# Third layer's attention: scores of batches 2 to 7 as three f32r products of upper and lower parts

## The chip, the cores and the metric

One core of a Trainium2 chip runs the whole program. The metric is device time in microseconds (us) for one execution, taken as the median of several. PE is TensorE (matmuls and transposes), DVE is VectorE, ACT is ScalarE, POOL is GpSimd, SP issues the transfers.

## The reference, cut to what matters

Four cross-attention layers run one after the other over x (8 batches x 256 rows x 256) and a context of 8 x 64 rows. The change lies in the last layer, which calls the function below twice, with its own weights each time, and then runs an MLP:

```python
def _cross_attention(q_in, kv_in, wq, bq, wk, bk, wv, bv, wo, bo, bias_k, bias_v):
    qh = (q_in @ wq + bq).reshape(b, q_len, H, K)        # 16 heads of 128
    kh = (kv_in @ wk + bk).reshape(b, t, H, K)           # 64 keys
    vh = (kv_in @ wv + bv).reshape(b, t, H, K)
    kh, vh = (each with one more row: bias_k, bias_v)
    logits = jnp.einsum('bqhk,bthk->bhqt', qh, kh) / sqrt(K)
    weights = jax.nn.softmax(logits, axis=-1)
    ctx = jnp.einsum('bhqt,bthk->bqhk', weights, vh).reshape(b, q_len, H * K)
    return ctx @ wo + bo

h = _layer_norm(x, ln1_scale, ln1_offset)
x = x + _cross_attention(h, xf_1, ...)                   # then the same with ln2 and the second weights
h = gelu(_layer_norm(x) @ w_fc1 + b_fc1) @ w_fc2 + b_fc2
return x + h
```

## The kernel before, in words

For each of the two attentions (a = 0, 1) the kernel first folds each head's weights into the context. `g3` (128 partitions x 2 halves of the 256 columns x 8 batches x 1024) is what a normalised row is multiplied with to give all 16 heads' scores against the 64 keys; `v3` is the same for the output. Only two large products are then left for each tile of 128 rows: scores, 128 x 256 by 256 x 1024, and output, 128 x 1024 by 1024 x 256. There are 16 tiles, two to a batch.

The function `attend` of each engine's program runs over these tiles in turns. Call turn n the body of `batch(i, ...)` for n = 2i + k. The engines do in turn n, in the order of the code:

- PE (L1184 on): `scores` of tile n+2 (L1159, four fp32 products of 512 columns, two instructions each, into four banks of PSUM that alternate by tile), `turn` of tile n (eight transposes of the weights, L1171), `turn_normed` of tile n+3 (transposes of the normalised rows, L1150), `rows_out` of tile n (L1180, 8 products of 256 columns).
- DVE: `stats` of tile n+4, `shifted` of tile n+2 (maximum L2002, the floor at zero L2004, subtraction L2005), `normed` of n+4 (L1994), `inverse` of n+2 (sum L2012, reciprocal L2013), `residual` of n (L2018).
- ACT: `copied` of tile n (transposed weights out of PSUM), `normed` of tile n+3 (transposed rows into `hT`), `weights` of n+2 (the exponential, L1226).
- POOL: `bias` of tile n (row plus output bias into `xb3`, L2313), `root3` of tile n+4 (L2089), `weights` of tile n+2 (times the reciprocal sum, L2307, 128 x 1024).

Each engine takes its instructions strictly in this order; semaphores tie the engines, with `wait(t, i, k)` for "step t of that tile is done". During the last eight turns of the second attention `feed` mixes in the first steps of the MLP: letters N (POOL: a root), A (ACT: upper parts of MLP weights), T (DVE, PE, ACT: one tile normalised, turned, copied), a (POOL: lower parts of MLP weights), X, x, C, c. In the turns with T, ACT's copies of the MLP's columns stand ahead of the exponential, and PE's transposes for them stand at the end of the turn.

A product "in parts" exists elsewhere in the kernel already: an fp32 matrix is held as an f32r upper part and an f32r remainder, and `PARTS = ((0, 0), (0, 1), (1, 0))` names the three products that are summed.

## Time and profile before

| | us |
|---|---|
| median of 3 runs | 1121.95 |
| lowest, highest | 1119.29, 1122.03 |
| span of the profiled execution | 1117.8 |
| median less that span | 4.15 |
| PE busy | 1043.6 (93%) |
| DVE busy | 725.0 (65%) |
| ACT busy | 601.4 (54%) |
| POOL busy | 451.9 (40%) |
| mean granted TensorE clock | 0.985 |

The span runs from the first to the last instruction of one profiled execution. An engine's busy time is the time in which at least one of its instructions ran; matmuls overlap, so the duration of one is longer than the distance to the next. The granted clock is 1 at 2.4 GHz and 0.5 at 1.2 GHz.

### The profile page before, as it was taken

To read this page: it belongs to the slowest core of one execution; us is meant where nothing else is said; L and a number is where in the kernel's file an instruction comes from. 1 tells how busy PE (TensorE), PEld (TensorE's weight loads), DVE (VectorE), ACT (ScalarE), POOL (GpSimd) and SP (SyncE) were. 2 spreads that over 40 slices of the span, in tenths; PEclk is the share of its full clock that TensorE was granted. 3 is DMA by queue.
4 is the path that set the end of the run, shared out by engine and by line. 5 is a ranking of instruction groups with operands and counts; after the bars stand their busy time and mean duration, and the time that the engine had idled before them with its cause. 6 is when DMAs were issued, how large, how long until landed. Compare 5 with 4: busy or idle time off the path is not lost.

```text
span 1117.8 us, 18511 instructions
## 1 busy us (share of the span) xinstructions
PE 1043.6 (93%) x6532; PEld 763.4 (68%) x6532; DVE 725.0 (65%) x1494; ACT 601.4 (54%) x1110; POOL 451.9 (40%) x436
## 2 busy tenths in 40 slices
PE   6889886799999989999999999999999999999998
PEld 4767764456665546777778866666788666667887
DVE  5868863567777734256478967666688776674553
ACT  3667765166665565455368742323587532346543
POOL 3768776434431123113034424334344243356241
PEclk9989999799999999999999999999999999999999
DMA  8010006777776021100023210000222200000000
GB/s 301 8 29 2 2 3 96 128 111 105 104 104 99 2 77 38 66 2 19 1 76 94 89 37 1 1 0 1 75 90 83 76 1 1 1 1 1 20 29 29
DMA packets 37152, 55.95 MB, mean 50 GB/s; under 512 B 12550, under 2 KB 29510, under 8 KB 34758
## 3 DMA queue, kind: packets, MB, share of 16 engines
q1 hardware_dynamic: 34998, 54.25, 21.8%
q8 instruction: 53, 0.87, 0.3%
q10 hardware_dynamic: 2064, 0.52, 0.2%
q14 instruction: 37, 0.30, 0.1%
HBM read 45.34 MB, written 9.18 MB: 49 GB/s over the span
## 4 chain that ended last, share of the span: by engine, by line
PE 69%; DVE 5%; ACT 3%; issue 2%; POOL 2%; DMA 1%; SPq 1%; ACTq 0%; DVEq 0%; POOLq 0%
PE ps L1180 9%; PE ps L900 8%; PE ps L1066 8%; PE ps L1159 7%; PE ps L970 5%; PE ps L851 4%; PE ps L1077 4%; PE ps L1087 4%; PE ps L818 4%; PE ps L752 3%; PE ps L971 3%; PE ps L832 2%; DVE nm L1748 2%; ACT pT L1223 1%; PE ps L870 1%
## 5 line engine op out<-in xcount | busy, mean ns | idle before, releaser
L1223 ACT ACTIVATE pT<-ps 128x512 f32<-128x512 f32 (+1 forms) x144 | 74.0, 558 | 150.9 <-PE ps L1171 119.1
L1748 DVE TENSOR_REDUCE nm<-ps 128x1 f32<-128x320 f32 x256 | 114.4, 486 | 54.1 <-PE ps L818 51.5
L1180 PE MATMUL ps<-v,pT 128*128 128x256 f32 x512 | 118.7, 385 | 7.0 <-DVE xr L2018 3.8
L2307 POOL TENSOR_TENSOR pn<-p,sm 128x1024 f32<-128x1024 f32 x32 | 60.9, 1904 | 151.5 <-DVE sm L2013 151.5
L2249 POOL TENSOR_TENSOR wl<-bun_m,wh 128x512 fp32r<-128x512 f32 x64 | 80.6, 1263 | 100.4 <-ACT wh L1223 100.4
L1159 PE MATMUL ps<-g,cT 128*128 128x512 f32 x256 | 114.8, 592 | 0.0
L1180 PEld LDWEIGHTS ps<-v,pT 128*128 128x128 f32 x512 | 94.6, 190 | 25.6 <-ACT pT L1223 11.9
L970 PE MATMUL ps<-wb,hid_high 128*128 128x512 f32 x256 | 97.0, 416 | 0.0
L1226 ACT ACTIVATE pT<-ps 128x512 f32<-128x512 f32 x160 | 85.3, 606 | 15.5 <-PE ps L832 15.3
L1226 ACT ACTIVATE p<-p 128x1024 f32<-128x1024 f32 (+1 forms) x64 | 68.5, 1070 | 41.5 <-DVE p L2005 40.0
L818 PE MATMUL ps<-ks,qs 97*128 97x320 bf16 x256 | 71.4, 311 | 15.1 <-DVE nm L1748 7.8
L1159 PEld LDWEIGHTS ps<-g,cT 128*128 128x128 f32 x256 | 48.2, 190 | 48.1 <-issue 46.9
L1833 DVE TENSOR_TENSOR hid_low<-hidf,hid_high 128x512 fp32r<-128x512 f32 x64 | 47.0, 735 | 42.9 <-ACT hid_high L1223 42.8
L971 PE MATMUL ps<-wb,hid_low 128*128 128x256 f32 x256 | 71.7, 280 | 0.0
L1425 ACT ACTIVATE hidf<-ps,vec 128x512 f32<-128x512 f32 x64 | 44.1, 689 | 43.5 <-PE ps L900 43.3
L2123 POOL TENSOR_TENSOR p<-p,mx 128x1024 f32<-128x1024 f32 x32 | 60.9, 1904 | 13.8 <-DVE mx L1691 13.8
L2265 POOL TENSOR_TENSOR xbm<-xr,row 128x256 f32<-128x256 f32 x32 | 23.5, 736 | 97.1 <-DVE xr L1860 92.2
L2012 DVE TENSOR_REDUCE sm<-p 128x16 f32<-128x1040 f32 x32 | 39.6, 1236 | 35.3 <-ACT p L1226 35.3
L2002 DVE TENSOR_REDUCE mx<-ps 128x16 f32<-128x1024 f32 x32 | 39.1, 1221 | 31.9 <-PE ps L1159 31.9
L970 PEld LDWEIGHTS ps<-wb,hid_high 128*128 128x128 f32 x256 | 48.1, 188 | 14.4 <-issue 4.8
L818 PEld LDWEIGHTS ps<-ks,qs 97*128 97x128 bf16 x256 | 23.2, 97 | 48.7 <-DVE nm L1748 25.2
L851 PE MATMUL ps<-pT,vt 128*32 128x256 f32 x768 | 48.1, 383 | 2.2 <-ACT oT L1223 2.2
(229 smaller groups left out, 2610.7 us busy)
## 6 DMA issues: line engine op xcount, KB each, us to landing
bun_m<-in_heads SPq DMA_DIRECT2D x32, 515.0 KB, 3.5
ks<-k_parts SPq DMA_DIRECT2D x48, 160.0 KB
qs<-q_parts SPq DMA_DIRECT2D x48, 128.0 KB
q_parts<-qp SPq DMA_DIRECT2D x8, 384.0 KB, 9.6
k_parts<-kp SPq DMA_DIRECT2D x8, 384.0 KB, 7.8
w<-in_w SPq DMA_DIRECT2D x2, 1024.0 KB, 4.8
xr<-in_x SPq DMA_DIRECT2D x1, 2048.0 KB, 15.9
out<-xr SPq DMA_DIRECT2D x16, 128.0 KB, 1.7
```

What stands on the lines that cost most here:

```text
L818: mm(ps[:, u % 2, 0:KEYS1], qs1[i % 3][0:MASK_ROW + 1, h, t * P:(t + 1) * P], ks1[i % 3][0:MASK_ROW + 1, h, :], start=True, stop=True).the ...
L851: last = mm(ps[32 * j:32 * j + 32, 5, 0:S], vt1[i % 2][:, c, h, :], p, start=c == 0, stop=c == 2)
L900: last = mm(ps[:, f % 2, :], w["wa"][a][:, kt, f * P:(f + 1) * P], w["x"][i % 2][b][:, kt, :], start=n == 0 and kt == 0, stop=n == len(PAR ...
L970: mm(ps[:, 2 + t, :], high, w["wb"][:, f, :, :].rearrange("p c d -> p (c d)"), start=f == 0, stop=False)
L971: last = mm(ps[:, 2 + t, 0:D], low, w["wb"][:, f, 0, :], start=False, stop=f == FT - 1)
L1066: last = mm(ps[:, bank, :], head_weights(m, a)["w" + name[0]][:, kt, :], cp3[b][:, kt, :], start=n == 0 and kt == 0, stop=n == len(PARTS) ...
L1159: last = mm(ps[:, 2 * t + c, :], hT[t][:, kt, :], g3[:, kt, bass.ds(b, 1), c * 512:(c + 1) * 512], start=kt == 0, stop=kt == KT - 1)
L1180: last = mm(o, pT3[half][:, n, :], v3[:, bass.ds(i, 1), 4 * half + n, :], start=half == 0 and n == 0, stop=half == 1 and n == 3)
L1223: return nc.scalar.activation(o, x, ACT.Identity, bias=bias, scale=scale)
L1226: return nc.scalar.activation(o, x, ACT.Exp, bias=bias, scale=scale)
L1748: v.tensor_reduce(nm1[i % 2][:, t, h:h + 1], ps[:, u % 2, 0:KEYS1], X, ALU.max, negate=True).then_inc(D1t["maxima"].sem, 1)
L2249: g.tensor_tensor(wl3[m % 2][:, cols], bun[m % BUNS][:, cols], wh3[m % 2][:, cols].bitcast(F32), ALU.subtract).then_inc(GH["low"].sem, 1)
```

## The change

The rows' transposes of batches 2 to 7 are kept as two f32r parts in `hs3`, laid over the memory of `cT`: ACT writes the upper part straight from PSUM, DVE subtracts it from PSUM for the lower (`normed_low`). `g3` of batch b is split as well: ACT copies its upper part into the place of batch b-2 (`g_high`, one half of the columns per turn, 128 x 1024), and POOL subtracts it from `g3` in place (`g_low`, also 128 x 1024). In POOL's turn n, `g_low` stands behind `weights`; PE's scores of batch b wait for the last `g_low` of that batch. With that, scores of batches 2 to 7 are 12 f32r products of 512 columns. Batches 0 and 1 stay fp32. The tile `xb3` goes: POOL adds the bias to the rows in place, as soon as the rows have been normalised.

```diff
--- before.py
+++ after.py
@@ -70,6 +70,7 @@
 BUNS = 3
 
 KEYS3 = H3 * SC
+PARTS3 = 2
 
 
 CONST = dict(ident=(0, P), quarter=(128, 4), parity=(132, 2), half=(134, 2), minus_half=(136, 1))
@@ -158,6 +159,9 @@
 
 
         xr = sb("xr", [P, NQ, D])
+        over_c = ExitStack()
+        hs3 = sb("hs3", [P, 2, 2, KT, P], F32R, where=over_c)
+        over_c.close()
         cT = sb("cT", [P, KT, C])
         cst = sb("cst", [P, NCONST])
         vec = sb("vec", [P, NVEC])
@@ -281,7 +285,10 @@
 
 
         late = ExitStack()
-        g3 = sb("g3", [P, KT, B, KEYS3], where=late)
+        over_g = ExitStack()
+        g3 = sb("g3", [P, KT, B, KEYS3], where=over_g)
+        over_g.close()
+        gs3 = sb("gs3", [P, KT, B, KEYS3], F32R, where=late)
         v3 = sb("v3", [P, B, HP, D], where=late)
         hn = [sb(f"hn{t}", [P, D], where=late) for t in range(2)]
         st3 = sb("st3", [P, 6], where=late)
@@ -289,7 +296,6 @@
         mx3 = [sb(f"mx3_{t}", [P, H3], where=late) for t in range(2)]
         sm3 = [sb(f"sm3_{t}", [P, H3], where=late) for t in range(2)]
         hT = [cT[:, t, 0:KT * P].rearrange("p (k n) -> p k n", k=KT) for t in range(2)]
-        xb3 = [cT[:, t, KT * P:KT * P + D] for t in range(2)]
         pT3 = [sb("pT3_0", [P, 4, P], where=late)]
         sb("beside_l2", [P, 72], where=late)
         bun_m3 = sb("bun_m3", [P, KT * F + FT * D], where=late)
@@ -401,9 +407,13 @@
 
 
         E3 = tallies("attn_pe", own_pe, normed=2, scores=2, turned_a=2, turned_b=2, out=2)
-        D3t = tallies("attn_dve", own_dve, stats=2, mean=2, eps=2, normed=2, max=2, floor=2, shifted=2, sum=2, inverse=2, rows=2)
-        A3 = tallies("attn_act", own_act, normed=2, weights=2, copied_a=2, copied_b=2)
-        G3 = tallies("attn_pool", own_pool, root=2, bias=2, weights=2)
+        D3t = tallies("attn_dve", own_dve, normed_low=2, stats=2, mean=2, eps=2, normed=2, max=2, floor=2, shifted=2, sum=2, inverse=2, rows=2)
+        A3 = tallies("attn_act", own_act, g_high=KT, normed=2, weights=2, copied_a=2, copied_b=2)
+        G3 = tallies("attn_pool", own_pool, g_low=KT, root=2, bias=2, weights=2)
+
+        def in_parts(t, a, b, k):
+
+            return t.at(a * (B - PARTS3) + b - PARTS3, k)
 
         def attn_end(t, a):
             return t.end((a + 1) * B)
@@ -1139,6 +1149,8 @@
                 def turn_normed(i, k, first=False):
                     wait(D3t["normed"], i, k)
                     wait(A3["normed"], i, k - 1)
+                    if i + (k - 1) // 2 >= PARTS3:
+                        pe.wait_ge(D3t["normed_low"].sem, in_parts(D3t["normed_low"], a, i + (k - 1) // 2, (k - 1) % 2))
                     if first:
                         for t in (DH["out"], AH["out"]):
                             pe.wait_ge(t.sem, t.end((a + 1) * H3))
@@ -1154,9 +1166,17 @@
                     t, b = k % 2, i + k // 2
                     wait(A3["normed"], i, k)
                     wait(D3t["shifted"], i, k - 2)
-                    for c in range(2):
+                    if b >= PARTS3:
+                        pe.wait_ge(D3t["normed_low"].sem, in_parts(D3t["normed_low"], a, b, t))
+                        pe.wait_ge(G3["g_low"].sem, in_parts(G3["g_low"], a, b, KT - 1))
+                        for c in range(2):
+                            for n, (p, q) in enumerate(PARTS):
+                                for kt in range(KT):
+                                    last = mm(ps[:, 2 * t + c, :], hs3[:, t, p, kt, :], gs3[:, kt, b if q else b - PARTS3, c * 512:(c + 1) * 512],
+                                              start=n == 0 and kt == 0, stop=n == len(PARTS) - 1 and kt == KT - 1)
+                    for c in range(0 if b >= PARTS3 else 2):
                         for kt in range(KT):
-                            last = mm(ps[:, 2 * t + c, :], hT[t][:, kt, :], g3[:, kt, bass.ds(b, 1), c * 512:(c + 1) * 512],
+                            last = mm(ps[:, 2 * t + c, :], hT[t][:, kt, :], g3[:, kt, b, c * 512:(c + 1) * 512],
                                       start=kt == 0, stop=kt == KT - 1)
                     last.then_inc(E3["scores"].sem, 1)
 
@@ -1195,6 +1215,7 @@
                             if move == "T":
                                 if k + 3 < left:
                                     wait(A3["normed"], i, k + 3)
+                                    pe.wait_ge(D3t["normed_low"].sem, in_parts(D3t["normed_low"], a, i + (k + 3) // 2, (k + 3) % 2))
                                 mlp_turn(0, tile, bank=6)
 
                 pe.wait_ge(D2["rows"].sem, D2["rows"].end(NQ))
@@ -1550,11 +1571,16 @@
                 def normed(i, k):
                     wait(E3["normed"], i, k)
                     wait(E3["scores"], i, k - 2)
-                    copy(hT[k % 2][:, :, :], ps[:, 6, 0:D].rearrange("p (k n) -> p k n", k=KT)).then_inc(A3["normed"].sem, 1)
+                    o = hs3[:, k % 2, 0, :, :] if i + k // 2 >= PARTS3 else hT[k % 2][:, :, :]
+                    copy(o, ps[:, 6, 0:D].rearrange("p (k n) -> p k n", k=KT)).then_inc(A3["normed"].sem, 1)
 
                 def weights(i, k):
                     wait(D3t["shifted"], i, k)
                     exp(p3[k % 2][:, :, :], p3[k % 2][:, :, :], scale=SCALE3).then_inc(A3["weights"].sem, 1)
+
+                def g_high(b, kt):
+                    wait(E3["scores"], b - PARTS3, 1)
+                    copy(gs3[:, kt, b - PARTS3, :], g3[:, kt, b, :]).then_inc(A3["g_high"].sem, 1)
 
                 def copied(i, k):
                     wait(E3["out"], i, k - 1)
@@ -1575,6 +1601,8 @@
                                 mlp_columns(0, t, bank=6)
                         if k + 2 < left:
                             weights(i, k + 2)
+                        if i + PARTS3 < B:
+                            g_high(i + PARTS3, k)
                         if a == 0 and i == B - 2:
                             rounded(H3, k)
                         for move, n in feed(a, i, k):
@@ -2012,10 +2040,16 @@
                     own3("sum", i, k, v.tensor_reduce(sm3[t][:, :], p3[t][:, :, :], X, ALU.add))
                     v.reciprocal(sm3[t][:, :], sm3[t][:, :]).then_inc(D3t["inverse"].sem, 1)
 
+                def normed_low(i, k):
+                    t = k % 2
+                    wait(A3["normed"], i, k)
+                    v.tensor_tensor(hs3[:, t, 1, :, :], ps[:, 6, 0:D].rearrange("p (k n) -> p k n", k=KT),
+                                    hs3[:, t, 0, :, :].bitcast(F32), ALU.subtract).then_inc(D3t["normed_low"].sem, 1)
+
                 def residual(i, k):
                     wait(E3["out"], i, k)
                     wait(G3["bias"], i, k)
-                    v.tensor_tensor(rows(i, k), ps[:, 7, 0:D], xb3[k % 2], ALU.add).then_inc(D3t["rows"].sem, 1)
+                    v.tensor_tensor(rows(i, k), ps[:, 7, 0:D], rows(i, k), ALU.add).then_inc(D3t["rows"].sem, 1)
 
                 def batch(i, left=NQ):
                     for k in range(2):
@@ -2028,6 +2062,8 @@
                                 mlp_normed(0, t)
                         if k + 4 < left:
                             normed(i, k + 4)
+                        if k + 3 < left and i + (k + 3) // 2 >= PARTS3:
+                            normed_low(i, k + 3)
                         if k + 2 < left:
                             inverse(i, k + 2)
                         residual(i, k)
@@ -2308,9 +2344,14 @@
                                     ).then_inc(G3["weights"].sem, 1)
 
                 def bias(i, k):
-                    wait(D3t["rows"], i, k - 2)
+                    wait(D3t["normed"], i, k)
                     settle(pool)
-                    g.tensor_tensor(xb3[k % 2], xq(i, k), vs3[:, :], ALU.add).then_inc(G3["bias"].sem, 1)
+                    g.tensor_tensor(xq(i, k), xq(i, k), vs3[:, :], ALU.add).then_inc(G3["bias"].sem, 1)
+
+                def g_low(b, kt):
+                    pool.wait_ge(A3["g_high"].sem, in_parts(A3["g_high"], a, b, kt))
+                    g.tensor_tensor(gs3[:, kt, b, :], g3[:, kt, b, :], gs3[:, kt, b - PARTS3, :].bitcast(F32), ALU.subtract
+                                    ).then_inc(G3["g_low"].sem, 1)
 
                 def batch(i, left=NQ):
                     for k in range(2):
@@ -2319,6 +2360,8 @@
                             root3(i, k + 4)
                         if k + 2 < left:
                             weights(i, k + 2)
+                        if i + PARTS3 < B:
+                            g_low(i + PARTS3, k)
                         if a == 0 and (i, k) in ((B - 2, 1), (B - 1, 0)):
                             low(H3, 1 - k)
                         for move, t in feed(a, i, k):
```

## Rows read from the trace of the kernel before

**Rows 1.** Page, part 4: the chain that ended last, shares by engine.
```profile
PE 69%; DVE 5%; ACT 3%; issue 2%; POOL 2%; DMA 1%; SPq 1%; ACTq 0%; DVEq 0%; POOLq 0%
```

**Rows 2.** Timeline of PE, first attention, turn 4: start, us, engine, line, out<-in, count.
```profile
694.99 3.60 PE L1159 MATMUL ps<-g,cT 128*128 128x512 f32 x8
...
699.77 3.72 PE L1180 MATMUL ps<-v,pT 128*128 128x256 f32 x16
```

**Rows 3.** Timeline of DVE in the same turn; in brackets idle time before, and releaser.
```profile
698.62 1.23 DVE L2002 TENSOR_REDUCE mx<-ps 128x16 f32<-128x1024 f32 x1 [1.89 <-PE ps L1159]
...
700.10 1.23 DVE L2005 TENSOR_TENSOR p<-ps,p 128x1024 f32<-128x1024 f32 x1
...
702.46 1.24 DVE L2012 TENSOR_REDUCE sm<-p 128x16 f32<-128x1040 f32 x1 [0.82 <-ACT p L1226]
```

**Rows 4.** Timeline of POOL in the same turn.
```profile
704.06 1.90 POOL L2307 TENSOR_TENSOR pn<-p,sm 128x1024 f32<-128x1024 f32 x1 [5.24 <-DVE sm L2013]
705.92 0.72 POOL L2313 TENSOR_TENSOR cT<-xr,vs 128x256 f32<-128x256 f32 x1
```

**Rows 5.** The chain that ended last in order of time: start, us, engine, line, count.
```profile
463.05 10.90 PE ps L900 x48
...
695.15 3.43 PE ps L1159 x8
```

**Rows 6.** Groups by line and form: busy us in total, mean ns, idle before.
```profile
L2232 POOL TENSOR_TENSOR xp_low<-xc,xp_high 128x1024 fp32r<-128x1024 f32 x4 | 9.5, 2386 | 25.9 <-DVE xp_high L1802 25.9
...
L1223 ACT ACTIVATE cp_high<-cT 128x1024 fp32r<-128x1024 f32 x1 | 1.1, 1059 | 0.0
...
L2018 DVE TENSOR_TENSOR xr<-ps,cT 128x256 f32<-128x256 f32 x32 | 11.8, 369 | 18.6 <-PE ps L1180 12.5 <-POOL cT L2313 6.0
```

**Rows 7.** Timelines of DVE, PE and POOL, first attention, turns 1 and 2.
```profile
676.61 0.46 DVE L2004 TENSOR_SCALAR p<-mx 128x16 f32<-128x16 f32 x1
...
678.31 3.60 PE L1159 MATMUL ps<-g,cT 128*128 128x512 f32 x8
...
674.44 1.90 POOL L2307 TENSOR_TENSOR pn<-p,sm 128x1024 f32<-128x1024 f32 x1 [2.91 <-DVE sm L2013]
676.30 0.73 POOL L2313 TENSOR_TENSOR cT<-xr,vs 128x256 f32<-128x256 f32 x1
...
681.06 1.91 POOL L2307 TENSOR_TENSOR pn<-p,sm 128x1024 f32<-128x1024 f32 x1 [3.53 <-DVE sm L2013]
```

**Rows 8.** Timelines of PE and ACT, second attention, turns 8 to 12.
```profile
958.17 3.60 PE L1159 MATMUL ps<-g,cT 128*128 128x512 f32 x8
...
975.06 3.60 PE L1159 MATMUL ps<-g,cT 128*128 128x512 f32 x8
...
993.49 3.60 PE L1159 MATMUL ps<-g,cT 128*128 128x512 f32 x8
...
975.96 1.07 ACT L1226 ACTIVATE p<-p 128x1040 f32<-128x1040 f32 x1
```

**Rows 9.** PE's longest idle time in the middle of the kernel, in PE's timeline.
```profile
196.59 0.71 PE L818 MATMUL ps<-ks,qs 97*128 97x320 bf16 x2 [5.92 <-DMA ks<-k_parts]
```

**Rows 10.** Stretches: from:to, length, busy PE PEld DVE ACT POOL, granted clock, DMA.
```profile
32.00:34.00 2.00, 1.97 (x34) 1.64 (x36) 0.94 (x1) 0.36 (x2) 2.00 (x2) 0.93 0.03 8
34.00:37.00 3.00, 3.00 (x20) 2.77 (x19) 2.40 (x6) 0.99 (x3) 1.59 (x2) 0.50 0.00 0
37.00:40.00 3.00, 2.85 (x40) 2.28 (x39) 2.97 (x3) 2.56 (x5) 1.11 (x2) 0.98 0.01 3
...
76.00:84.00 8.00, 7.91 (x48) 6.48 (x49) 4.03 (x5) 4.99 (x11) 2.67 (x3) 0.50 0.00 0
...
192.00:194.00 2.00, 0.00 (x0) 0.00 (x0) 0.57 (x1) 0.00 (x0) 1.84 (x3) 1.00 1.22 139
194.00:196.00 2.00, 0.00 (x0) 0.00 (x0) 0.00 (x0) 0.00 (x0) 1.71 (x3) 0.54 0.71 100
...
204.00:206.00 2.00, 1.34 (x6) 0.35 (x4) 1.57 (x4) 1.47 (x3) 0.00 (x0) 0.90 0.81 98
```

## Prediction

> **What bounds the kernel now.** I read the chain that ended last first: PE carries 69% of it [rows 1], and in both attentions it consists of L1159 and L1180 by turns. Then I laid the timelines of four engines over one turn. PE goes without a gap through 3.43 us of scores [rows 5] and 1.35 us of transposes up to 699.77, then 3.56 us of output [rows 2]; from turn 2 to turn 4 pass 694.99 - 678.31 = 16.68 us [rows 2, 7], 8.34 a turn. The other engines wait for PE.
>
> What the totals hide is the length of the softmax chain behind one tile's scores. With T for the start of the scores in a turn: maximum at T+3.63, subtraction at T+5.11, sum at T+7.47 [rows 3], POOL's product with the reciprocals at T+9.07, and the next POOL instruction can start at T+10.93 [rows 4]. So each tile's chain ends in the following turn. It costs nothing before, since PE transposes these weights only two turns after it computed the scores. POOL idles 5.24 us of a turn [rows 4], but it does so in front of this product.
>
> **Scores in parts.** Fp32 scores take 3.43 us a tile (x8 in the chain) [rows 5]. The MLP's f32r products of the same shape, 512 columns with new weights each, take 10.90/48 = 0.227 us [rows 5]. Twelve are 2.73 us: 0.70 us less a tile, and a turn of PE falls from 8.34 to 7.64. Batches 2 to 7 are 12 tiles, 24 in both attentions: 16.8 us, if PE goes on without gaps. The last product's tail of 0.17 us behind its distance stays.
>
> **The split of the rows.** ACT's copy only changes its target's type. DVE's subtraction is 128 x 256 from PSUM, 0.37 us as L2018 [rows 6], between `normed` and the sum. DVE waits there for the exponential, 0.82 us [rows 3], and that hides it; uncovered it would be 0.37 on the chain below. The bounds for the whole item are 0 and 12 x 0.37 = 4.4 us.
>
> **The split of g3.** Each of turns 0 to 11 of an attention gets one ACT copy of 128 x 1024, 1.06 us, and one POOL subtraction of 128 x 1024 into f32r, 2.39 us [rows 6]. The ACT copy stands behind the exponential, which ends at T+7.4, and has nothing behind it before the next turn's transposes. POOL's load is no trouble either: of 5.24 us idle [rows 4] the shorter turn leaves 4.5. The place in the order is the trouble. PE's scores in turn n+1 (n odd) are the first of a new batch and wait for the `g_low` of turn n. This stands in POOL's queue behind the product with the reciprocals, which ends the chain of the tile whose scores PE computed in the same turn n. So PE can't begin turn n+1 before that whole chain has run, and one `g_low` on top of it.
>
> **The price of one such wait.** With the shorter scores everything moves up by 0.70: the product on POOL would start at T+8.37. One thing pushes it back. The even turn's `g_low` begins some 10.2 us after the start of that turn and ends 12.65 us after it, at T+5.0 of the odd turn, and DVE's floor (L2004, a tensor_scalar, due at T+4.2) falls into it. Such a collision shows in [rows 7]: the floor was issued at 676.61 while POOL's bias ran from 676.30 to 677.03, and took 0.46; in turn 4 all that lies between maximum and subtraction is 0.25 [rows 3]. So subtraction starts at about T+5.10, like before, and POOL's product at T+9.06. Plus 1.86, plus 2.39, plus some 0.04: PE starts the next turn at T+13.35 in place of T+8.34. That leaves PE idle for 13.35 - 7.64 = 5.7 us.
>
> The Trainium skill, SBUF — State Buffer, section "Who interferes with whom", has the rule for the collision: DVE in a two-port mode and GpSimd exclude each other for a whole instruction, and tensor_scalar can be such a DVE instruction. The trace agrees (0.46 us there). By that rule an added GpSimd instruction of 2.39 us can block DVE for as long.
>
> **The sum without the clock.** Attention 1: two turns take 7.64 + 13.35 = 20.99 in place of 16.68, +4.3, for turns 2 to 11, five pairs: +21.6. The first wait is longer. In turn 1 DVE is still behind: POOL's product of turn 0 starts at 674.44 and that of turn 1 at 681.06 [rows 7]. `g_low` fills 676.30 to 678.69 and holds the floor from 676.61 until then; subtraction 678.75, exponential 680.0, sum 681.1, product 682.7, `g_low` 684.6 to 686.95. Turn 2 starts at 687.0 instead of 678.31 [rows 7]: +8.7. Turns 12 and 13 have fast scores and no wait: -1.4. Sum +28.9.
>
> Attention 2: +8.7 and three pairs of 4.3 (12.9) alike. In turn 9 `feed` puts ACT's columns ahead of the exponential, and these wait for PE's transposes at the end of the turn: the exponential comes at 975.96, 0.90 us behind the start of PE's turn 10 at 975.06 [rows 8]. That was harmless; now it is in the chain. With PE's work of turn 9 ending at T+7.87 the exponential starts at T+8.77, sum T+9.87, product T+11.5, `g_low` ends at T+15.7: the pair takes 7.64 + 15.75 = 23.4 for 975.06 - 958.17 = 16.89 [rows 8], +6.5. In turn 11 the root for the MLP stands behind turn 10's `g_low` too, which pushes the transposes to about T+10 and the end to T+17.9: 8.0 + 17.9 = 25.9 for 993.49 - 975.06 = 18.43, +7.5. With -1.4 for turns 12 and 13: +34.2.
>
> Both: +63. Bounds: without collisions of the floor and with everything else hidden, 12 waits less 0.7 each, +55; with 0.7 more each, +71.
>
> **The clock.** Before, PE is never idle in the attentions for more than 2 us, and the clock stays at 1. A wait of 5.7 us and more, twelve times, is new. The nearest row is PE's idle time of 5.92 us up to 196.59 [rows 9]: the clock is 1 until 194, 0.54 over 194 to 196, so it fell some 3.5 us into the idle time, and it came back only after 204 [rows 10]. Ours would be at 1.2 GHz (0.5) when PE resumes. How long it stays there: around 34 it fell after a poor stretch and was back at 37, five us after PE had resumed at 32; the one at 76 to 84 stayed at half for over 8 us of nearly full work [rows 10]. I take 5 us at half, since our work is dense from the resumption on, as after 32: 2.5 us lost a wait, 12 x 2.5 = 30. The lost time lies on the path, since PE's even turn is paced by PE. Bounds: 0 if the clock doesn't fall, 12 x 4.9 = 59 by the long row.
>
> The Trainium skill, TensorE: Matmul & The Clock Gate, section "HAM oscillation — how this bites in real kernels", describes a kernel that waits in every tile and starts each cold again; that rule speaks against this change, and the rows above agree with it for one wait (0.54 and then 0.50).
>
> **In place of `xb3`** POOL adds the bias to the rows in place behind the wait for `normed`, four turns old in its start: no instruction more or less, 0. SP issues nothing new. PE's added waits for the rows' lower parts are met: that subtraction ends some 1 us before the scores that use it.
>
> **Forecast.** The profiled execution: 1117.8 + 63 + 30 = 1210.8; the median stood 4.15 above the span: 1215 us, with 1200 to 1232 as its own range. Chance 0.75.
>
> **Rivals.**
> - The clock holds. The waits are as priced, but PE stays at 2.4 GHz: 1121.95 + 63 = 1185, between 1177 and 1193. For it: the idle times of up to 2 us in the attentions leave the clock at 1. Against: the row of 5.92 us. Chance 0.12.
> - The clock is worse, each resumption like that at 76: 1121.95 + 63 + 59 = 1244, 1232 to 1250. Chance 0.06.
> - The other side: PE stays the bound. The lower parts would have to be ready when PE gets to the new batch, that is `g_low` would have to end before T+7.64 of the odd turn. It decides at that point; I find T+13.3. POOL's 5.24 us of idle time would hold 2.39 us, if it ran there. Only if POOL's order or the semaphore's count were not what I read does the price turn to a gain: 1121.95 - 16.8 = 1105 (1101 to 1112). Chance 0.04.
> - It doesn't do what it says: twelve f32r products take as long as eight fp32 instructions, and low parts come in time: 1122. With the waits it would be some 1121.95 + 63 + 30 + 10 x 2 x 0.7 = 1229, inside the forecast's range. For the first, 0.03.
>
> **How the numbers follow.** The likeliest case gives 1215. The range takes in the first rival and the second up to 1244: 1176 to 1244, with 0.93 of the chances laid out, less some room for my sizes. A change of 0.3%, 3.4 us, is about what a measurement of this kernel can tell from none. Faster 0.04, same 0.03, slower 0.93.
>
> **What would show it.** In the changed trace: twelve f32r matmuls of L1159's successor in 2.7 us in a turn at full clock; PE idle for 5 to 6 us ahead of the scores of turns 4, 6, ... 12, 8.7 ahead of those of turn 2, released by POOL's subtraction into `g`; 20 to 23 us a pair of turns; POOL's subtraction starting right behind its product; the granted clock at 0.5 for some us after each wait, and nowhere else new. If PE shows no idle time there, the order was misread and the time is 1105. If the pairs take 21.0 us with a clock of 1, the first rival holds.

## The result, and the profile after

The changed kernel takes 1214.12 us (median of 4 runs, 1211.31 to 1220.13); the kernel before, run beside it, 1121.57 (1119.29 to 1122.03). The ratio is 1.082, 95% interval 1.078 to 1.086. The forecast was 1215 us, slower. The profiled execution is the longest of the four, 1220.13 us, with a span of 1218.2.

In the page of the changed kernel the chain that ended last (shares of the span by engine) has 57% of PE for 69% in [rows 1], 10% of POOL for 2%, and 10% of "issue", time in which the engine waited for nothing that the profile shows, for 2%. Below are two groups of the page (busy us, mean ns, idle time before and its releaser) and the longest entry of the view of waits (us in total, times, longest):

```profile
PE 57%; issue 10%; POOL 10%; DVE 4%; ACT 2%; DMA 1%; SPq 1%; POOLq 0%; ACTq 0%; DVEq 0%
...
L1175 PE MATMUL ps<-gs,hs 128*128 128x512 f32 x288 | 99.4, 510 | 75.8 <-POOL gs L2353 75.8
...
L2353 POOL TENSOR_TENSOR gs<-g,gs 128x1024 fp32r<-128x1024 f32 x24 | 56.7, 2361 | 0.0
```
```profile
PE ps L1175 <- POOL gs L2353: 75.8, 12, 8.6
```

L1175 is the f32r scores, L2353 is `g_low`. PE waits for it twelve times, 75.8 us in all: six batches in each attention, as the order of the queues has it.

The timeline of PE in the first attention, turns 2 to 5 (start, us, engine, line; L1200 is the output):

```profile
693.00 5.46 PE L1175 MATMUL ps<-gs,hs 128*128 128x512 f32 x12 [8.55 <-POOL gs L2353]
...
699.79 3.72 PE L1200 MATMUL ps<-v,pT 128*128 128x256 f32 x16
703.16 3.11 PE L1175 MATMUL ps<-gs,hs 128*128 128x512 f32 x12
...
707.45 3.72 PE L1200 MATMUL ps<-v,pT 128*128 128x256 f32 x16
716.55 5.46 PE L1175 MATMUL ps<-gs,hs 128*128 128x512 f32 x12 [5.38 <-POOL gs L2353]
...
723.50 3.72 PE L1200 MATMUL ps<-v,pT 128*128 128x256 f32 x16
726.87 3.12 PE L1175 MATMUL ps<-gs,hs 128*128 128x512 f32 x12
```

To be seen: the odd turn's scores (703.16) go on without a gap, and the next even turn starts 13.39 us after them. The same twelve products take 3.11 us without a wait ahead of them and 5.46 behind this one (4.34 to 5.46 behind the twelve waits). The windows of the same stretch tell why (us; busy us and count of PE, PEld, DVE, ACT, POOL; granted clock; DMA share; GB/s):

```profile
692.00:698.00 6.00, 5.00 (x12) 3.96 (x13) 0.00 (x0) 0.00 (x0) 2.05 (x3) 0.50 0.00 0
698.00:704.00 6.00, 5.91 (x31) 4.97 (x30) 4.91 (x8) 3.38 (x5) 0.06 (x1) 0.95 0.00 0
704.00:716.00 12.00, 7.07 (x36) 5.61 (x34) 7.01 (x15) 3.38 (x5) 9.16 (x6) 0.99 0.01 2
716.00:722.00 6.00, 5.45 (x13) 4.21 (x14) 0.00 (x0) 0.00 (x0) 1.59 (x3) 0.50 0.00 0
```

When PE resumes, the granted clock is 0.50, that is 1.2 GHz of 2.4, and it stays there for some three to five and a half us, behind each of the twelve waits.

POOL in turn 3 shows the queue order at work. The first `g_low` is that of the even turn 2, the second the one that PE waits for; it starts right behind the product (L2343), and PE resumes 0.14 us after it (716.41 to 716.55):

```profile
703.94 1.91 POOL L2343 TENSOR_TENSOR pn<-p,sm 128x1024 f32<-128x1024 f32 x1 [9.89 <-DVE sm L2041]
705.81 2.36 POOL L2353 TENSOR_TENSOR gs<-g,gs 128x1024 fp32r<-128x1024 f32 x1
...
712.21 1.90 POOL L2343 TENSOR_TENSOR pn<-p,sm 128x1024 f32<-128x1024 f32 x1 [2.84 <-DVE sm L2041]
714.07 2.34 POOL L2353 TENSOR_TENSOR gs<-g,gs 128x1024 fp32r<-128x1024 f32 x1
```

DVE's floor (L2032) under such a `g_low`, in turn 1 and in turn 3:

```profile
682.59 2.07 DVE L2032 TENSOR_SCALAR p<-mx 128x16 f32<-128x16 f32 x1
...
706.30 1.23 DVE L2030 TENSOR_REDUCE mx<-ps 128x16 f32<-128x1024 f32 x1 [1.36 <-PE ps L1175]
707.56 0.65 DVE L2032 TENSOR_SCALAR p<-mx 128x16 f32<-128x16 f32 x1
708.24 1.22 DVE L2033 TENSOR_TENSOR p<-ps,p 128x1024 f32<-128x1024 f32 x1
```

Its 16 elements a partition take 2.07 us in turn 1, since it ends with POOL's subtraction (682.28 to 684.62), and 0.65 in turn 3, to 708.21, with the one that began at 705.81. The subtraction behind it, from PSUM, keeps its 1.22 us beside POOL's next instruction, the bias; e9 below has it beside `g_low` itself (705.37, 1.23 us).

Where the 100.4 us between the spans of 1218.2 and 1117.8 went: the last output of attention 1 on PE, in the kernel before and then in the changed one:

```profile
784.61 3.72 PE L1180 MATMUL ps<-v,pT 128*128 128x256 f32 x16 [0.31 <-ACT pT L1223]
```
```profile
833.45 3.72 PE L1200 MATMUL ps<-v,pT 128*128 128x256 f32 x16 [0.31 <-ACT pT L1244]
```

These are 48.8 us. Of them 6.0 were there before the attention began (its first scores start at 658.9 for 652.94): this one execution had a lower clock in stages where nothing was changed (0.86 for 1.00 from 100 to 150 us, 0.74 for 0.83 from 190 to 230). So attention 1 costs 42.9 and all behind it 51.5.

### The profile page after: what moved, and what is told of

Same layout as the page of the kernel before. It is cut to its first block, busy times and chain, and to the rows that moved or that the text cites. A ratio compares the mean times of both kernels' runs of the same rounds, so it can differ in the third digit from the quotient of the medians.

```text
span 1218.2 us, 18809 instructions
## 1 busy us (share of the span) xinstructions
PE 1066.4 (88%) x6628; PEld 805.4 (66%) x6628; DVE 742.8 (61%) x1518; ACT 624.1 (51%) x1134; POOL 508.1 (42%) x460
## 4 chain that ended last, share of the span: by engine, by line
PE 57%; issue 10%; POOL 10%; DVE 4%; ACT 2%; DMA 1%; SPq 1%; POOLq 0%; ACTq 0%; DVEq 0%
PE ps L910 7%; PE ps L1076 7%; PE ps L1175 6%; PE ps L980 5%; POOL gs L2353 4%; PE ps L861 4%; PE ps L1087 4%; PE ps L1097 4%; POOL pn L2343 4%; PE ps L828 3%; PE ps L762 3%; PE ps L1200 2%; PE ps L981 2%; PE ps L842 2%; DVE nm L1776 2%
## 5 line engine op out<-in xcount | busy, mean ns | idle before, releaser
L1175 PE MATMUL ps<-gs,hs 128*128 128x512 f32 x288 | 99.4, 510 | 75.8 <-POOL gs L2353 75.8
L2343 POOL TENSOR_TENSOR pn<-p,sm 128x1024 f32<-128x1024 f32 x32 | 60.9, 1904 | 190.3 <-DVE sm L2041 190.3
L1175 PEld LDWEIGHTS ps<-gs,hs 128*128 128x128 f32 x288 | 71.1, 253 | 96.6 <-issue 79.9
L1200 PE MATMUL ps<-v,pT 128*128 128x256 f32 x512 | 118.7, 385 | 8.0 <-DVE xr L2052 4.4
L1200 PEld LDWEIGHTS ps<-v,pT 128*128 128x128 f32 x512 | 94.6, 190 | 26.6 <-ACT pT L1244 12.9
L1247 ACT ACTIVATE pT<-ps 128x512 f32<-128x512 f32 x160 | 85.3, 606 | 15.5 <-PE ps L842 15.2
L1247 ACT ACTIVATE p<-p 128x1024 f32<-128x1024 f32 (+1 forms) x64 | 68.2, 1068 | 45.6 <-DVE p L2033 44.7
L2301 POOL TENSOR_TENSOR xbm<-xr,row 128x256 f32<-128x256 f32 x32 | 23.5, 736 | 97.0 <-DVE xr L1888 92.1
L2040 DVE TENSOR_REDUCE sm<-p 128x16 f32<-128x1040 f32 x32 | 39.6, 1236 | 30.7 <-ACT p L1247 30.7
L2353 POOL TENSOR_TENSOR gs<-g,gs 128x1024 fp32r<-128x1024 f32 x24 | 56.7, 2361 | 0.0
```

The lines of the kernel that those rows point to most:

```text
L1175: last = mm(ps[:, 2 * t + c, :], hs3[:, t, p, kt, :], gs3[:, kt, b if q else b - PARTS3, c * 512:(c + 1) * 512], start=n == 0 and kt == 0, ...
L1200: last = mm(o, pT3[half][:, n, :], v3[:, bass.ds(i, 1), 4 * half + n, :], start=half == 0 and n == 0, stop=half == 1 and n == 3)
L1247: return nc.scalar.activation(o, x, ACT.Exp, bias=bias, scale=scale)
L2343: g.tensor_tensor(pn3[t][:, :, :], p3[t][:, :, 0:SC], sm3[t][:, :].unsqueeze(2).broadcast_to([P, H3, SC]), ALU.mult).then_inc(G3["weights" ...
L2353: g.tensor_tensor(gs3[:, kt, b, :], g3[:, kt, b, :], gs3[:, kt, b - PARTS3, :].bitcast(F32), ALU.subtract).then_inc(G3["g_low"].sem, 1)
```

## The experiments

In each diff `-` is the changed kernel unless another is named. Every run stands beside runs of the kernel before on the same chip.

**e1: both halves of the split ahead of the softmax chain.** If the place in the queues is the cause, this removes the waits.

```diff
@@ ACT, batch()
                     for k in range(2):
+                        if i + PARTS3 < B:
+                            g_high(i + PARTS3, k)
                         copied(i, k)
...
-                        if i + PARTS3 < B:
-                            g_high(i + PARTS3, k)
@@ POOL, batch()
                     for k in range(2):
+                        if i + PARTS3 < B:
+                            g_low(i + PARTS3, k)
...
-                        if i + PARTS3 < B:
-                            g_low(i + PARTS3, k)
```

> The changed kernel with ACT's upper copy and POOL's lower subtraction of g3 moved to the head of their turns; nothing else is touched. My theory (place in POOL's order): the subtraction of an odd turn then ends some 5 us into the turn, before PE's 7.64 us are over, PE has no gap, the clock stays at 1, and the 24 faster scores are left: 1121.6 - 16.8 = 1105 us (1101 to 1111). Rival A (the splitting costs by its load on ACT, DVE and POOL or by collisions, wherever it stands): above 1121. Rival B (f32r products gain nothing here): 1120 to 1123.

Measured: 1134.23 us (1132.96 to 1136.05), ratio 1.010 (1.008 to 1.012). 80 of the 93 us are back, so the place of the two halves of the split caused most of the loss. The 17 us of gain are not there: of the expectations the first rival came, costs of load or collisions wherever the split stands. PE, DVE and POOL in a turn:

```profile
703.09 3.00 PE L1175 MATMUL ps<-gs,hs 128*128 128x512 f32 x12 [0.34 <-DVE hs L2046]
...
711.35 2.98 PE L1175 MATMUL ps<-gs,hs 128*128 128x512 f32 x12 [0.35 <-DVE hs L2046]
```
```profile
703.29 1.24 DVE L2040 TENSOR_REDUCE sm<-p 128x16 f32<-128x1040 f32 x1 [0.46 <-ACT p L1247]
...
707.39 1.77 DVE L2032 TENSOR_SCALAR p<-mx 128x16 f32<-128x16 f32 x1
...
711.55 1.24 DVE L2040 TENSOR_REDUCE sm<-p 128x16 f32<-128x1040 f32 x1 [0.46 <-ACT p L1247]
```
```profile
704.90 1.91 POOL L2343 TENSOR_TENSOR pn<-p,sm 128x1024 f32<-128x1024 f32 x1 [2.85 <-DVE sm L2041]
706.76 2.36 POOL L2353 TENSOR_TENSOR gs<-g,gs 128x1024 fp32r<-128x1024 f32 x1
```

At the head of POOL's turn `g_low` is in effect right behind the product of the turn before. There it holds DVE's floor until 709.16, as the exclusion of DVE and POOL that the prediction priced would have it. That closes a loop of its own: sum 703.29, product 704.90, `g_low` 706.76, floor to 709.16, shifted scores 709.19, exponential, next sum 711.55. It is 8.26 us long with no step of PE in it, where PE's work is 7.64 and was 8.34 [rows 2, 7]: nearly all of the 0.70 us a tile goes into it. In attention 2 the turns with the MLP's rows take up to 11.96 us.

**e2: only POOL's order, `g_low` between the root and the product.**

```diff
@@ POOL, batch()
                             root3(i, k + 4)
+                        if i + PARTS3 < B:
+                            g_low(i + PARTS3, k)
                         if k + 2 < left:
                             weights(i, k + 2)
-                        if i + PARTS3 < B:
-                            g_low(i + PARTS3, k)
```

> The changed kernel with POOL's subtraction ahead of its product with the reciprocals, but ACT's copy still behind the exponential. Theory: PE now waits for subtraction, exponential, ACT's copy and POOL's subtraction: next turn at T+10.2 in place of T+13.2, so PE idles 2.5 us in place of 5.4. If the clock holds through 2.5 us: some 19 us above the kernel before, 1141 (1130 to 1150). If it falls there too, another 12 x 2.4: 1165 to 1170. Rival (POOL's order does not matter, its load does): 1214.

Measured: 1171.1 us (1169.73 to 1177.79), ratio 1.044 (1.041 to 1.047), just above the 1165 to 1170 that stood for waits that still cost clock. POOL's order alone gives 43 us back; the 37 us between this kernel and e1 are the price of ACT's place once POOL's is cured. ACT's copy remains behind the exponential, and `g_low` waits for it, so PE idles for 2.5 us. PE's scores behind three such waits:

```profile
706.84 4.48 PE L1175 MATMUL ps<-gs,hs 128*128 128x512 f32 x12 [2.48 <-POOL gs L2353]
...
726.43 3.00 PE L1175 MATMUL ps<-gs,hs 128*128 128x512 f32 x12 [2.46 <-POOL gs L2353]
...
744.49 4.57 PE L1175 MATMUL ps<-gs,hs 128*128 128x512 f32 x12 [2.50 <-POOL gs L2353]
```

With the same idle time the clock fell at two of these and held at one. Four of this kernel's twelve waits are longer (5.31 to 5.48 us), and all four are followed by slow scores (4.82 to 5.46 us). Of the eight of 2.45 to 2.87 us five are (4.47 to 4.59 us), and three are not (2.99 to 3.01 us).

**e3: only ACT's order, `g_high` at the head of its turn** (the ACT half of e1's diff).

> The changed kernel with ACT's upper copy at the head of its turn, POOL's order as in the change. Theory: the copy is not what PE waits for, since POOL is busy with the product until after it; so no change: 1214 (1208 to 1220), PE's idle time of about 5.3 us a pair of turns stays. Rival (ACT's copy is the late link): 1105 to 1145.

Measured: 1215.52 us (1214.05 to 1219.38), ratio 1.083 (1.080 to 1.085), no change. The waits stay at 75.9 us, twelve times. In the order of the change ACT's place costs nothing, since POOL's queue is the later of the two links; e2 against e1 shows that it is the next one.

**e4: the waits kept, PE kept busy in them** by six fp32 products of 512 columns into the bank that the scores overwrite.

```diff
@@ PE, scores()
+                        if t == 0:
+                            for n in range(FILL):
+                                mm(ps[:, 2 * t, :], ident, v3[:, 0, 0:2, :].rearrange("p h d -> p (h d)"), start=True, stop=True)
                         pe.wait_ge(G3["g_low"].sem, in_parts(G3["g_low"], a, b, KT - 1))
```

> The changed kernel with six added fp32 products of 512 columns (0.86 us each, 5.1 us together, results overwritten) in each of the twelve places in which PE waits. The chain on the other engines stays as long. If the clock's fall costs what I put down, 2.0 to 2.7 us a wait, it holds now and the time falls by 24 to 30 us: 1187 (1182 to 1194), granted clock at 1 in the attentions. If the slow scores after the wait are due to something else than idle time, 1214.

Measured: 1191.49 us (1189.69 to 1196.65), ratio 1.062 (1.059 to 1.064): 22.6 us less than the changed kernel, with 0.972 to 0.983 as mean clock for 0.942 to 0.951. Two even turns of it (L1179 is the scores there, and the rest of the wait stands in brackets):

```profile
709.83 3.06 PE L1179 MATMUL ps<-gs,hs 128*128 128x512 f32 x12 [0.30 <-POOL gs L2357]
...
730.89 3.06 PE L1179 MATMUL ps<-gs,hs 128*128 128x512 f32 x12 [0.30 <-POOL gs L2357]
```

The pair takes 21.06 us at full clock, where 23.55 pass in the changed kernel (693.00 to 716.55). This splits the loss. By the medians, each with some 3 or 4 us either way, 22.6 of 92.6 us are clock and 70 waiting, less what the shorter scores give. The traces are sharper, since the stages before the attentions can be left out: from the first scores of attention 1 to the end the kernel before takes 464.9 us, e4 533.0 and the changed kernel 559.3. One wait of e4 was not covered (2.54 us idle, scores of 4.62 us, about 1.6 lost). That makes some 66.5 us of waiting and 27.9 of clock.

**e5: the scores of batches 2 to 7 as fp32 products of the upper parts.** All splits and waits stay; the lower parts are left out of the scores, so that they are coarser.

```diff
@@ PE, scores()
-                            for n, (p, q) in enumerate(PARTS):
-                                for kt in range(KT):
-                                    last = mm(ps[:, 2 * t + c, :], hs3[:, t, p, kt, :], gs3[:, kt, b if q else b - PARTS3, c * 512:(c + 1) * 512],
-                                              start=n == 0 and kt == 0, stop=n == len(PARTS) - 1 and kt == KT - 1)
+                            for kt in range(KT):
+                                last = mm(ps[:, 2 * t + c, :], hs3[:, t, 0, kt, :].bitcast(F32), gs3[:, kt, b - PARTS3, c * 512:(c + 1) * 512].bitcast(F32),
+                                          start=kt == 0, stop=kt == KT - 1)
```

> The changed kernel with all its waits and splits, but the scores of batches 2 to 7 as four fp32 products of the upper parts (the lower parts' products are left out, so what is computed is less exact). Theory: fp32 scores are 0.70 us longer in each of 24 turns, and all of it lies on the path: 1214 + 17 = 1231 us (1225 to 1236). Rival (f32r products gain nothing, or the gain is swallowed by the wait): 1214.

Measured: 1228.4 us (1223.86 to 1231.16), ratio 1.097 (1.095 to 1.100): 14.3 us above the changed kernel. So the f32r products do save time on the path, and the rival in which they save nothing falls. The expectation had all of the 16.8 us on the path, 0.70 in each of 24 turns; the trace has less, 10.3 us from the first scores to the end (569.6 for 559.3). DVE, POOL and PE in turn 3 (L2031 is the floor there, L2352 `g_low`, L1174 the scores):

```profile
702.39 0.18 DVE L2031 TENSOR_SCALAR p<-mx 128x16 f32<-128x16 f32 x1
...
700.09 2.35 POOL L2352 TENSOR_TENSOR gs<-g,gs 128x1024 fp32r<-128x1024 f32 x1
...
697.49 3.60 PE L1174 MATMUL ps<-gs,hs 128*128 128x512 f32 x8
```

With the longer scores the floor is due at 702.39, when `g_low` is all but over (702.44), and takes 0.18 us; it ends 5.08 us after the start of the scores. With the shorter ones it is due earlier and is held, to 5.05 us after that start (708.21 - 703.16). In attention 1 such a turn takes 13.41 to 13.68 us to the next scores in e5 and 13.24 to 13.80 in the changed kernel. So in the odd turns that a wait follows the faster product saves next to nothing (in attention 2 the five of them are 1.4 us longer in e5, all together). The other 14 turns give 9.8 us at full clock.

**e6: on the kernel before, only the bias added in place.**

```diff
@@ DVE, residual()
-                    v.tensor_tensor(rows(i, k), ps[:, 7, 0:D], xb3[k % 2], ALU.add)
+                    v.tensor_tensor(rows(i, k), ps[:, 7, 0:D], rows(i, k), ALU.add)
@@ POOL, bias()
-                    wait(D3t["rows"], i, k - 2)
+                    wait(D3t["normed"], i, k)
-                    g.tensor_tensor(xb3[k % 2], xq(i, k), vs3[:, :], ALU.add)
+                    g.tensor_tensor(xq(i, k), xq(i, k), vs3[:, :], ALU.add)
```

> The kernel before with only one part of the change: POOL adds the bias to the rows in place behind the wait for the normalised rows, and the tile for the sum goes. Theory: no time, 1121.3 (1118 to 1125). Rival (the freed wait lets POOL run ahead and collide with DVE, or shortens the end): more than 3 us either way.

Measured: 1121.83 us for 1123.02, ratio 0.999 (0.997 to 1.001). This part costs nothing that can be measured.

**e8: ACT's columns for the MLP behind the exponential**, in attention 2.

```diff
@@ ACT, batch()
                             normed(i, k + 3)
+                        if k + 2 < left:
+                            weights(i, k + 2)
                         for move, t in feed(a, i, k):
...
-                        if k + 2 < left:
-                            weights(i, k + 2)
```

> The changed kernel with ACT's columns of the MLP behind the exponential in the four turns that have them. Theory: turn 9 of the second attention loses the 2.9 us by which the exponential waited for PE's transposes; turn 11 little, since DVE's sum stands there behind the MLP's row, which waits for POOL. 1211 (1206 to 1214). Rival (the exponential sets both): 6 us less, 1208 or below.

Measured: 1208.47 us (1204.25 to 1213.74), ratio 1.079 (1.076 to 1.082), 5.7 us less than the changed kernel, between the two expectations, and by its interval of about 3 us either way the median doesn't tell them apart. The trace does (scores of turns 10 and 12):

```profile
1053.05 5.46 PE L1175 MATMUL ps<-gs,hs 128*128 128x512 f32 x12 [5.28 <-POOL gs L2353]
...
1077.84 5.18 PE L1175 MATMUL ps<-gs,hs 128*128 128x512 f32 x12 [5.34 <-POOL gs L2353]
```

Turns 8 and 9 take 23.5 us (from 1029.57) for 25.6 in the changed kernel, turns 10 and 11 24.8 for 30.7, together 8.0 us less. So the rival holds: ACT's order sets both pairs, and the second more than the first.

**e9: `g_high` at the head of ACT's turn, `g_low` behind bias and root, and there only after DVE's floor.**

```diff
@@ POOL, batch() (ACT as in e3)
                             root3(i, k + 4)
+                        if i + PARTS3 < B:
+                            wait(D3t["floor"], i, k + 2)
+                            g_low(i + PARTS3, k)
                         if k + 2 < left:
                             weights(i, k + 2)
-                        if i + PARTS3 < B:
-                            g_low(i + PARTS3, k)
```

> Of the kernel with both steps ahead (1134 us) the trace shows turns of 8.25 us in a closed loop: DVE's floor waits 1.6 us for POOL's subtraction to end, and PE waits 0.35 us for the rows' lower part. Here POOL's subtraction stands behind bias and root and waits for the floor. Theory (the collision makes the loop): the floor takes 0.2 us again, turns come down to 7.9 to 8.1, the time to 1120 (1113 to 1128). Rival (the loop is POOL's load, whatever collides): 8.25 or longer, 1134 or above.

Measured: 1123.46 us (1119.84 to 1131.83), ratio 1.002 (0.999 to 1.004). DVE's floor and PE's turn:

```profile
705.15 0.18 DVE L2032 TENSOR_SCALAR p<-mx 128x16 f32<-128x16 f32 x1
```
```profile
700.83 3.02 PE L1175 MATMUL ps<-gs,hs 128*128 128x512 f32 x12
...
708.50 3.02 PE L1175 MATMUL ps<-gs,hs 128*128 128x512 f32 x12
```

The floor takes 0.18 us instead of 1.77, and a turn of PE 7.67 without a gap, against 8.26 in e1. The rival in which POOL's load makes the loop is out, since POOL's work is the same; so it was the collision. The edit moves `g_low` behind bias and root and adds the wait; what each does alone was not tried. Two things keep the time at that of the kernel before: turn 1 of each attention takes 12.2 us for 8.9, since PE waits 2.11 us for `normed_low`, and turns 9 to 12 of attention 2 take 8.5, 11.7, 11.9 and 8.8 us.

**e10: e9, and on DVE `normed_low` right behind the shifted scores, `normed` behind the sum.**

```diff
@@ DVE, against e9
-                        if k + 4 < left:
-                            normed(i, k + 4)
                         if k + 3 < left and i + (k + 3) // 2 >= PARTS3:
                             normed_low(i, k + 3)
-                        if k + 2 < left:
-                            inverse(i, k + 2)
+                        inverse(i, k + 2, k + 2 < left, k + 4 < left)
@@ inverse(), between the sum and the reciprocal
+                    if more:
+                        normed(i, k + 2)
```

> The same, and DVE subtracts the rows' lower part right behind the scores' subtraction and normalises the next rows only behind the sum. Theory: PE no longer waits for the lower part, turns of 7.65 to 7.8 us, 1113 (1107 to 1120), faster than the kernel before. Rival (DVE and POOL together need more than 7.9 us a turn in any order): 1120 and above.

Measured: 1119.24 us (1115.39 to 1124.46), ratio 0.998 (0.996 to 1.000); 1113 (1107 to 1120) was expected. The turns of attention 1 are the 7.67 us that the theory had; turns 10 to 12 of attention 2 still take 12.0, 12.1 and 9.1 us. POOL, DVE, PE and ACT there (L1822 normalises the MLP's rows, L895 transposes them on PE, the ACT line adds their columns, L1247 is the exponential):

```profile
975.81 2.34 POOL L2354 TENSOR_TENSOR gs<-g,gs 128x1024 fp32r<-128x1024 f32 x1
...
975.87 2.43 DVE L1822 TENSOR_SCALAR hnm<-xr,mvm 128x256 f32<-128x256 f32 x1
978.22 0.41 DVE L2050 TENSOR_TENSOR hs<-ps,hs 128x256 fp32r<-128x256 f32 x1
...
978.73 0.66 PE L895 MATMUL ps<-cst,hnm 128*128 128x128 f32 x2 [3.69 <-DVE hs L2050]
979.04 5.30 PE L1175 MATMUL ps<-gs,hs 128*128 128x512 f32 x12
...
979.43 0.81 ACT L1244 ACTIVATE xc<-ps,vec 128x128 f32<-128x128 f32 x2 [7.52 <-PE ps L895]
980.13 1.06 ACT L1247 ACTIVATE p<-p 128x1040 f32<-128x1040 f32 x1
```

A second tensor_scalar of DVE, L1822, is held by `g_low` for 2.43 us; PE's transposes wait for the `normed_low` behind it, ACT's columns for these, the exponential for the columns, and POOL's next product for the exponential. The scores were complete long before. Behind PE's 3.69 us of idle time its clock is at half as well (5.30 us).

**e11: e10, and the columns behind the exponential** (e8's diff on top).

> The kernel with rows late (1119 us), and ACT's columns of the MLP behind the exponential. In its trace turns 10 to 12 of the second attention take 12.0, 12.1 and 9.1 us, since DVE's row for the MLP (tensor_scalar) waits up to 2.4 us for POOL's subtraction. Theory: the exponential is not what is late there, so only some 2 us: 1117 (1114 to 1120).

Measured: 1109.43 us (1107.8 to 1114.44) for 1123.02, ratio 0.987 (0.984 to 0.991). It is faster than both kernels. ACT and PE in the same turns:

```profile
974.06 1.07 ACT L1247 ACTIVATE p<-p 128x1040 f32<-128x1040 f32 x1 [1.57 <-DVE p L2033]
```
```profile
976.83 0.41 PE L895 MATMUL ps<-cst,hnm 128*128 128x128 f32 x2 [1.33 <-DVE hs L2050]
```

The exponential follows the shifted scores directly, PE idles 1.33 us instead of 3.69, and turns 10 to 12 take 9.5, 9.5 and 7.9 us where e10 has 12.0, 12.1 and 9.1. Those 6.4 us are most of the 9.8 between the two medians. Expected was 1117 (1114 to 1120), on the theory that the exponential is not what is late in these turns. That was wrong: it is, here as in e8.

**e12: e11, and the MLP's rows (L1822) ahead of the floor**, that is before `g_low` may start.

```diff
@@ DVE, against e11
-                            shifted(i, k + 2)
-                        for move, t in feed(a, i, k):
-                            if move == "T":
-                                mlp_normed(0, t)
+                            shifted(i, k + 2, lambda: [mlp_normed(0, t) for move, t in feed(a, i, k) if move == "T"])
```

> The same, and DVE's row for the MLP between maximum and floor, ahead of POOL's subtraction in place of behind its start. Theory: it no longer collides, turns 10 to 12 take 8 to 9 us, 7 to 8 us less: 1110 (1106 to 1115). Rival (POOL's added work in these turns sets them, whatever collides): 1116 to 1119 as without it.

Measured: 1110.51 us (1109.15 to 1113.47), ratio 0.988 (0.985 to 0.991), the same as e11. The time agrees with the expectation, its reason doesn't: against e11 the step gained nothing that the medians show. L1822 does fall from 2.45 to 0.8 us, and turn 10 from 9.5 to 7.9, but turns 11 and 12 stay at 9.5 and 7.9: `g_low` starts later for it, and PE waits 0.85 us for that in turn 11.

## Why the prediction was right

**The order on POOL.** The prediction rests on one reading: `g_low` of an odd turn stands behind the product that ends the chain of the tile scored in the same turn. The trace has twelve waits with that releaser, and of the moves ACT's alone gives nothing back (e3), POOL's alone 43 us (e2) and both 80 (e1): POOL's place is the link that decides, as predicted, and ACT's, which the prediction took for harmless, is the next behind it. The rival in which PE stays the bound needed lower parts in time; even when they are (e1), it comes to 1134 and not 1105, since the floor then sits behind `g_low`. Only with that cured too (e9 to e11) is part of the gain seen.

**The size of a wait.** From an odd turn's start to the next even one 13.35 us were predicted, 13.39 and 13.24 (726.87 to 740.11) came, and 13.53 to 13.80 in the later turns of attention 1. The pair without the clock was 20.99, and e4 shows 21.06. The first wait was put at 8.7 us later than before: PE was at 693.00 in this execution, which is 687.0 as predicted plus the 6.0 from earlier stages. The steps in between held as well: in turn 3 the subtraction starts at T+5.08 (708.24 - 703.16) where T+5.10 was taken, and POOL's product at T+9.05 (712.21 - 703.16) for T+9.06.

**Attention 2.** Turns 8 and 9 took 25.6 us (1035.52 to 1061.12) where 23.4 + 2.5 were predicted. Turns 10 and 11 took 30.7 for 25.9 + 2.5, so this term was 2.3 too small. The timeline of DVE, PE and ACT in turn 11:

```profile
1082.77 0.41 DVE L2022 TENSOR_SCALAR hn<-xr,mv 128x255 f32<-128x255 f32 x1 [1.12 <-POOL mv L2125]
1083.10 0.42 DVE L2046 TENSOR_TENSOR hs<-ps,hs 128x256 fp32r<-128x256 f32 x1
...
1083.61 0.41 PE L895 MATMUL ps<-cst,hnm 128*128 128x128 f32 x2 [3.88 <-DVE hs L2046]
1091.81 5.46 PE L1175 MATMUL ps<-gs,hs 128*128 128x512 f32 x12 [7.78 <-POOL gs L2353]
...
1084.76 1.06 ACT L1247 ACTIVATE p<-p 128x1040 f32<-128x1040 f32 x1
```

I had the MLP's transposes at T+10, held by the root behind `g_low`. They came at T+11.76 (1083.61 - 1071.85). The root of the rows themselves stands even further back in POOL's queue, DVE's `normed` waits 1.12 us for it, `normed_low` stands behind `normed`, and PE's transposes behind that. I had called PE's waits for the rows' lower parts met; in this turn one was not, and e10 shows the same path. What makes it dear is the place of ACT's columns ahead of the exponential: without it the two turns take 24.8 us (e8).

**The scores.** 2.73 us a tile was right for the timeline (3.0 to 3.1 with the tail). The 16.8 us of saving were counted for a PE without gaps. Behind waits less comes, and the sum had this right, with the subtraction at T+5.10 "like before" in an odd turn: the floor's collision takes the 0.70 us back, and e5's trace shows it. The rival with 1229 us counted both turns of each pair and so was some 7 us too high. Without the waits 13.6 of the 16.8 us came (e11).

**The clock.** The mechanism was right at every wait. Even turns of attention 1 took 10.16, 10.32, 8.89, 9.55, 9.94 and 10.01 us where they take 7.57 to 7.62 in e4, at full clock: 13.3 us lost, 2.2 a wait where 2.5 were taken, 15 in all. Attention 2 lost 14.5 by the same comparison, which makes 27.8 for the kernel, as the 27.9 from the stretches of e4; the 30 of the sum was some 2 us too high. The price of one wait lies between 1.3 and 2.8 us. The rival in which the clock holds is out: its time is nearly that of e4, 1191, and 1177 to 1193 was its range.

The Trainium skill, TensorE: Matmul & The Clock Gate, section "HAM oscillation — how this bites in real kernels", says that a kernel which waits in each of its tiles starts every tile cold. This trace agrees in all twelve cases (clock 0.50 when PE resumes).

**The sum.** Predicted +28.9 + 15 for attention 1 and +34.2 + 15 behind it, 93.1; the profiled execution shows 42.9 and 51.5, 94.4. By kind, 63 of waiting and 30 of clock were predicted, and some 66.5 and 27.9 came: the waits were priced too low, in turns 10 and 11 above all, and the clock too high. That the total came out within 1.3 us, and the median on the forecast's 1215, is in part luck. The median rose by 92.6. My way from span to median was wrong, though it did no harm: I added 4.15 us to the span of the kernel before, while the changed kernel's own time stands 1.93 above its span. The 4.15 was mostly scatter between executions of the kernel before (1119.29 to 1122.03), whose times stand 1.8 above their spans wherever both are on record (1120.08 for 1118.3).

## What to carry to other kernels

Before an operation is put into an in-order queue, ask what stands ahead of it there and whose consumer it feeds: 2.4 us of work on an engine with 5 us of slack in a turn cost 93 us in all, because it stood behind the end of a chain that its own consumer had started. When such work is moved, look a second time at what it now collides with, since e1 swapped one wait for a closed loop of 8.26 us; a place behind the floor and the release of two more orders (e10, e11) then brought 13.6 of the 16.8 us counted. A faster PE product is worth what the slowest loop beside it leaves: next to nothing in the odd turns of the changed kernel (e5) and in e1. So lay that loop out first.

## What was not expected of the hardware

- The clock fell at five of eight waits of only 2.45 to 2.87 us, and held at three (e2). In the attentions of the kernel before, idle times of up to 1.9 us had left it at 1. But in e9 it fell behind 2.11 us (scores of 4.58 us) and behind 1.88 us (an output of 5.38 us for 3.69), and held behind the same 2.11 us in attention 2 (3.00 us). In both it still stood at 1 when PE resumed and fell within the next four us (0.60 and 0.59 as their mean). So the length of the last idle time alone doesn't tell; what does was not found out.
- A DVE tensor_scalar on 16 elements a partition took 0.18 us in e9 and 0.65, 1.77 or 2.07 under POOL's subtraction; one on 256 took up to 2.45 (0.76 in e12, ahead of `g_low`, and 0.41 alone). Tensor_reduce (1.22 to 1.24) and the subtraction from PSUM (1.22, 1.23) kept their times beside the same POOL instruction. The size of the DVE instruction said nothing of its cost; that of the POOL instruction under way did. The Trainium skill, SBUF — State Buffer, section "Who interferes with whom", has tensor_scalar among the operations that can take the shared ports, and tensor_reduce on this chip and instructions with at most one input in SBUF outside those modes among those that can't; all these rows agree.
